# Attention scores from six part products, two heads side by side in TensorE's rows

## The reference

```python
mod = (silu(c) @ wmod).reshape(4, 6, 1, 128)           # sa, ca, ga, sb, cb, gb
h = layernorm(x) * (1 + ca) + sa
Q, K, V = split_heads(h @ W_q.T), split_heads(h @ W_k.T), split_heads(h @ W_v.T)
Q, K = rope(Q), rope(K)
score = einsum('bnqd,bnkd->bnqk', Q, K) / sqrt(8)       # causal: -inf above the diagonal
attn = softmax(score)
x = x + ga * (attn @ V).reshape(4, 1024, 128) @ W_o.T
h = layernorm(x) * (1 + cb) + sb
# shared expert + the two best of 7 routed experts per token, by softmax of h @ wr.T + rb
x = x + gb * moe(h)
```

## Time and profile before

| | us |
|---|---|
| median of three runs | 922.52 |
| the three runs | 930.70, 922.52, 921.49 |
| the profiled execution | 927.8 |
| its span, first to last instruction | 926.1 |
| ahead of the attention's first maxima | 66.1 |
| attention, quads 0 to 15 | 461.3 (95.84 to 557.12) |
| behind the attention | 369.0 |

### The profile page before, as it was taken

The page is one execution under the profiler, slowest core; times in us unless marked ns, Lnnn a source line. Parts: engine busy times, 40 slices in busy tenths (PEclk is TensorE's granted clock), DMA queues, the critical chain, the costliest instruction groups (busy, mean ns, idle before and its releaser), DMA issues.

```text
span 926.1 us, 17554 instructions
## 1 busy us (share of the span) xinstructions
PE 788.9 (85%) x5168; PEld 442.1 (48%) x5168; DVE 625.0 (67%) x1970; ACT 510.4 (55%) x969; POOL 312.4 (34%) x491
## 2 busy tenths in 40 slices
PE   3988999999999999999999997650884778999990
PEld 2551333333333333333333356540764667999880
DVE  5999678998989989998989654720592222333353
ACT  3770366666767666666667778321422444666650
POOL 1347122122111222111221114075014766666562
PEclk9995589999999999999999997795897999999995
DMA  7480311323212332113330195021112222222524
GB/s 200 117 236 23 76 29 26 53 53 53 40 21 47 53 53 53 28 28 53 53 53 3 31 181 117 3 73 41 32 40 60 66 63 65 65 67 65 152 88 142
DMA packets 59051, 62.62 MB, mean 68 GB/s; under 512 B 9097, under 2 KB 50697, under 8 KB 56649
## 3 DMA queue, kind: packets, MB, share of 16 engines
q1 hardware_dynamic: 53218, 50.04, 25.0%
q0 software_dynamic: 4480, 9.64, 2.9%
q10 hardware_dynamic: 1264, 1.84, 0.6%
HBM read 37.55 MB, written 23.55 MB: 66 GB/s over the span
## 4 chain that ended last, share of the span: by engine, by line
PE 66%; DVE 10%; another core or an unknown queue 7%; ACT 6%; issue 5%; DMA 2%; SPq 1%; POOL 1%; ACTq 1%; DVEq 0%; POOLq 0%
PE ps L1492 15%; PE ps L1545 15%; PE ps L1570 14%; PE ps L1726 6%; PE ps L1737 5%; PE ps L1747 2%; DVE junk L1082 2%; PE ps L1633 2%; PE ps L1522 2%; DVE leftmax L1086 1%; PE ps L1641 1%; DMA qa<-mparts 1%; ACT rows L856 1%; SPq L582 1%
## 5 line engine op out<-in xcount | busy, mean ns | idle before, releaser
L835 ACT ACTIVATE probs<-ps 128x1024 f32<-128x1024 f32 (+3 forms) x384 | 295.1, 813 | 181.0 <-PE ps L1570 180.6
L1082 DVE CUSTOM_DVE_ANT_0 junk<-ps,tri 128x128 f32<-128x128 f32 (+3 forms) x512 | 221.6, 486 | 31.0 <-PE ps L1492 28.9
L1492 PE MATMUL ps<-ka,qa 72*128 72x512 bf16 (+3 forms) x768 | 224.1, 348 | 3.6 <-DVE rowmax L1082 2.3
L668 POOL TENSOR_SCALAR_AFFINE_SELECT probs<-probs 128x512 f32<-128x512 f32 x128 | 81.1, 634 | 380.2 <-ACT probs L835 380.2
L1570 PE MATMUL ps<-qa,ka 75*128 75x512 bf16 (+3 forms) x768 | 192.7, 334 | 1.6 <-DMA qa<-mparts 1.5
L1545 PE MATMUL ps<-probs,v 128*32 128x512 f32 (+3 forms) x1536 | 166.5, 506 | 1.8 <-POOL probs L668 1.8
L1086 DVE TENSOR_REDUCE leftmax<-ps 128x1 f32<-128x512 f32 x256 | 162.4, 682 | 7.4 <-PE ps L1492 7.3
L1492 PEld LDWEIGHTS ps<-ka,qa 72*128 72x128 bf16 x768 | 67.2, 99 | 167.6 <-DVE rowmax L1082 65.5
L1570 PEld LDWEIGHTS ps<-qa,ka 75*128 75x128 bf16 x768 | 71.8, 100 | 81.4 <-ACT probs L835 28.8
L735 POOL DMA_INDIRECT routed_results_scratch<-y_s,s_dest x76 | 76.2, 1003 | 61.7 <-issue 56.6
L676 POOL DMA_INDIRECT slot_rows_scratch<-rows,slot x64 | 62.6, 978 | 91.6 <-DVE slot L1283 73.1
(11 more groups left out here) (183 smaller groups left out, 1003.1 us busy)
## 6 DMA issues: line engine op xcount, KB each, us to landing
qa<-q_parts_scratch SPq DMA_DIRECT2D x48, 192.0 KB
slot_rows_scratch<-cst SPq DMA_DIRECT2D x1, 5396.0 KB, 34.3
srow<-slot_rows_scratch SPq DMA_DIRECT2D x76, 71.0 KB
ka<-k_parts_scratch SPq DMA_DIRECT2D x32, 128.0 KB
q_parts_scratch<-qk_parts SPq DMA_DIRECT2D x12, 256.0 KB, 4.6
k_parts_scratch<-qk_parts SPq DMA_DIRECT2D x12, 256.0 KB, 5.4
ka<-k_parts_scratch SPq DMA_DIRECT2D x16, 192.0 KB
xs<-in_x SPq DMA_DIRECT2D x4, 512.0 KB, 10.3
```

The lines of the kernel that those rows point to most:

```text
L668: nc.gpsimd.affine_select(out=p, in_=p, compare_op=ALU.is_ge, fill=0.0, base=0, pattern=[[0, HQ], [1, T]], channel_multiplier=-1).then_inc ...
L835: nc.scalar.activation(probs[s % 4][:, 2 * h:2 * h + 2, 0:CH - q0], ps[:, 2 * h:2 * h + 2, q0:CH], ACT.Exp, scale=SCALE).then_inc(s_exp, 1)
L1082: last = V.tensor_tensor_reduce(out=junk[:, bank - 5, at:at + w], in0=src, in1=tri[:, CH - w:CH], scale=1.0, scalar=LOW, op0=ALU.add, op1= ...
L1492: last = MM(ps[:, bank, at:at + w], qa[m][0:KR, h * S + q * T:h * S + (q + 1) * T], ka[m][0:KR, h * S + k0:h * S + k0 + w], start=True, st ...
```

## The change

Six of the nine pairs of parts stay: hi by all three, mid by two, the rest by one (`RUNS`), so KR = 48 and KM = 51. The pairs mid by rest, rest by mid and rest by rest are left out of the scores. To have each run of q parts against a run of k parts in rising order, k's parts stand reversed in the scratch.

Head 2j + g of a quad now stands at rows 64 g of `qa` and `ka`, columns j x 1024: two heads share the columns, one in rows 0 to 50, one in rows 64 to 114. The products of a pair of heads follow each other, in the order that changes the half of the rows each time. `PIECES` is ordered so that the same bank of two heads comes twice in a row, and `ring_plan` puts the second into the slot of the first. A quad is loaded by 12 DMAs instead of 8, the shift rows by 6 instead of 3, the ones rows by 6 instead of 3. Maxima are stored by g first, so that the shift rows of one half lie together.

```diff
-KR = NP * NP * DK
+RUNS = ((0, NP), (0, 2), (0, 1))
+KR = sum(b - a for a, b in RUNS) * DK
 KM = KR + NP
+HG = 64
+HC = HQ // 2
-PIECES = [(h, bank) for h in range(HQ) for bank in HEAD_BANKS]
+PIECES = [(2 * j + g, bank) for j in range(HC) for bank in HEAD_BANKS for g in range(2)]
@@ ring_plan
-        slot = next((s for end, s in slots if at < end), NS * SLOTS - 1)
+        if not (kind == "max" and p % 2 and plan and plan[-1][1:] == ("max", off, p - 1)):
+            slot = next((s for end, s in slots if at < end), NS * SLOTS - 1)
@@ buffers
-            qa[m] = sb(f"qa{m}", [KM, HQ * S], BF16, at=att)
-            ka[m] = sb(f"ka{m}", [KM, HQ * S], BF16, at=att)
+            qa[m] = sb(f"qa{m}", [128, HQ * S], BF16, at=att)
+            ka[m] = sb(f"ka{m}", [128, HQ * S], BF16, at=att)
@@ ones rows
-                sp.dma_start(ka[m][KR:KM, :], ones_d.bitcast(BF16)).then_inc(s_ones, 16)
+                for g in range(2):
+                    sp.dma_start(ka[m][g * HG + KR:g * HG + KM, 0:HC * S], ones_d.bitcast(BF16)).then_inc(s_ones, 16)
@@ spill
-                        dst = scr[b * NG:(b + 1) * NG, p, :, :].rearrange("g r s -> r g s")
+                        at = NP - 1 - p if w else p
+                        dst = scr[b * NG:(b + 1) * NG, at, :, :].rearrange("g r s -> r g s")
@@ load_quad
-                w = NP * DK
-                for j in range(NP):
-                    sp.dma_start(qa[m][j * w:(j + 1) * w, :], q[0:w, :]).then_inc(s_qk_in[m], 16)
-                    mid = (j + 1) * w - j * DK
-                    sp.dma_start(ka[m][j * w:mid, :], k[j * DK:w, :]).then_inc(s_qk_in[m], 16)
-                    if j:
-                        sp.dma_start(ka[m][mid:(j + 1) * w, :], k[0:j * DK, :]).then_inc(s_qk_in[m], 16)
+                for g in range(2):
+                    at = g * HG
+                    for first, stop in RUNS:
+                        rows_in = (stop - first) * DK
+                        q0, k0 = first * DK, (NP - stop) * DK
+                        dst_q = qa[m][at:at + rows_in, 0:HC * S].rearrange("r (j s) -> r j s", j=HC)
+                        dst_k = ka[m][at:at + rows_in, 0:HC * S].rearrange("r (j s) -> r j s", j=HC)
+                        sp.dma_start(dst_q, q[g, q0:q0 + rows_in, :, :]).then_inc(s_qk_in[m], 16)
+                        sp.dma_start(dst_k, k[g, k0:k0 + rows_in, :, :]).then_inc(s_qk_in[m], 16)
+                        at += rows_in
@@ load_shift
-                for p in range(NP):
-                    sp.dma_start(qa[m][KR + p:KR + p + 1, :].rearrange("o (a t) -> o a t", t=T),
-                                 mparts[m][:, p, :]).then_inc(s_m_in[m], 16)
+                for g in range(2):
+                    for p in range(NP):
+                        row = g * HG + KR + p
+                        sp.dma_start(qa[m][row:row + 1, 0:HC * S].rearrange("o (a t) -> o a t", t=T),
+                                     mparts[m][g * HC * TB:(g + 1) * HC * TB, p, :]).then_inc(s_m_in[m], 16)
@@ bank_maxima
                 h, parts = PIECES[what]
+                h = h % 2 * HC + h // 2
@@ row_scores
-                    last = MM(ps[:, bank, at:at + w], qa[m][0:KR, h * S + q * T:h * S + (q + 1) * T],
-                              ka[m][0:KR, h * S + k0:h * S + k0 + w], start=True, stop=True)
+                    last = MM(ps[:, bank, at:at + w], qa[m][g0:g0 + KR, c0 + q * T:c0 + (q + 1) * T],
+                              ka[m][g0:g0 + KR, c0 + k0:c0 + k0 + w], start=True, stop=True)
@@ body on TensorE
-                    for h in range(HQ):
-                        if h % 2 == 0 and not (first and s == 0):
-                            pe.wait_ge(s_exp, n * (2 * NS) + 2 * s + h // 2 - 1)
-                        last = MM(ps[:, h, q0:CH], ka[m][0:KM, h * S + kb * T:h * S + (kb + 1) * T],
-                                  qa[m][0:KM, h * S + c * CH + q0:h * S + (c + 1) * CH], start=True, stop=True)
-                        if h % 2:
-                            last.then_inc(s_scores, 1)
-                            ring_entries(s * SLOTS + h // 2)
+                    for pair in range(HC):
+                        if not (first and s == 0):
+                            pe.wait_ge(s_exp, n * (2 * NS) + 2 * s + pair - 1)
+                        for g in ((1, 0) if group[0] == 0 else (0, 1)):
+                            at = pair * S
+                            last = MM(ps[:, 2 * pair + g, q0:CH],
+                                      ka[m][g * HG:g * HG + KM, at + kb * T:at + (kb + 1) * T],
+                                      qa[m][g * HG:g * HG + KM, at + c * CH + q0:at + (c + 1) * CH], start=True, stop=True)
+                            group[0] = g
+                        last.then_inc(s_scores, 1)
+                        ring_entries(s * SLOTS + pair)
```

More of the change, by code:

```diff
@@ L482, in load_quad @@
                 n, m = quad(i, r), r % 3
-                q = qs_d[bass.ds(n, 1), :, :, :].rearrange("n p (d h) s -> (n p d) (h s)", h=HQ)
-                k = ks_d[bass.ds(n, 1), :, :, :].rearrange("n p (d h) s -> (n p d) (h s)", h=HQ)
-                w = NP * DK
-                for j in range(NP):
-                    sp.dma_start(qa[m][j * w:(j + 1) * w, :], q[0:w, :]).then_inc(s_qk_in[m], 16)
-                    mid = (j + 1) * w - j * DK
-                    sp.dma_start(ka[m][j * w:mid, :], k[j * DK:w, :]).then_inc(s_qk_in[m], 16)
-                    if j:
-                        sp.dma_start(ka[m][mid:(j + 1) * w, :], k[0:j * DK, :]).then_inc(s_qk_in[m], 16)
+                q = qs_d[n].rearrange("p (d j g) s -> g (p d) j s", j=HC, g=2)
+                k = ks_d[n].rearrange("p (d j g) s -> g (p d) j s", j=HC, g=2)
+                for g in range(2):
[8 more added lines that the diff above has]
+                        at += rows_in
             def load_shift(i, r):
@@ L1500, in ring_write @@
                     if what == 0:
-                        pe.wait_ge(s_qk_in[m], (third(i, r + off) + 1) * ((3 * NP - 1) * 16))
+                        pe.wait_ge(s_qk_in[m], (third(i, r + off) + 1) * (2 * 2 * len(RUNS) * 16))
                     last = row_scores(m, bank, what)
@@ L1525, in _ @@
             pe.wait_ge(s_v_free, 2 * B)
-            pe.wait_ge(s_ones, 16 * 3)
+            pe.wait_ge(s_ones, 16 * 3 * 2)
             for k, (kind, off, what) in enumerate(PRE):
@@ L1553, in body @@
                 rbase = ring_base(i, r)
-                pe.wait_ge(s_m_in[m], (third(i, r) + 1) * (16 * NP))
-                ks = [0]
+                pe.wait_ge(s_m_in[m], (third(i, r) + 1) * (16 * 2 * NP))
+                ks, group = [0], [None]
                 def ring_entries(slot):
@@ L1562, in ring_entries @@
                         ring_write(i, r, 5 + ring_bank(i, r, k), kind, off, what)
+                        group[0] = PIECES[what][0] % 2 if kind == "max" else None
                         ks[0] += 1
                 for s, (c, kb, q0) in enumerate(STEPS):
-                    for h in range(HQ):
-                        if h % 2 == 0 and not (first and s == 0):
-                            pe.wait_ge(s_exp, n * (2 * NS) + 2 * s + h // 2 - 1)
-                        last = MM(ps[:, h, q0:CH], ka[m][0:KM, h * S + kb * T:h * S + (kb + 1) * T],
-                                  qa[m][0:KM, h * S + c * CH + q0:h * S + (c + 1) * CH], start=True, stop=True)
-                        if h % 2:
-                            last.then_inc(s_scores, 1)
-                            ring_entries(s * SLOTS + h // 2)
+                    for pair in range(HC):
[9 more added lines that the diff above has]
+                        ring_entries(s * SLOTS + pair)
                     if s >= 2:
@@ L1798 @@
         cos.astype(np.float32), sin.astype(np.float32), np.eye(128, dtype=np.float32), tri, cst,
-        np.full((NP, HQ * S // 2), 0x3F803F80, np.uint32).view(np.float32),
+        np.full((NP, HC * S // 2), 0x3F803F80, np.uint32).view(np.float32),
     ]
```

1 line of the change is left out of this document (added).

## The result

The changed kernel is slower. The median of four runs is 961.1 us (959.3 to 964.9), beside 924.5 us (921.5 to 930.7) for the kernel before: a ratio of 1.039, interval 1.033 to 1.046. The prediction said 895 us, at most 921.

A forecast was written before the change was run, and what follows sets the result against it. TensorE was taken to bound the kernel, VectorE 2.5 us behind. Ahead +1, quad 0 -4, 13 settled quads from 28.39 to 27.0 us, last two -7: -28.1 us, from 922.5 to 895 us, range 879 to 921.

The forecast's parts named there:

- The overlap: Score products of two heads in different row halves run fully at once; L1570 falls from 7.9 to 4.0 us a quad.
- TensorE below VectorE: In a settled quad TensorE's sum becomes 20.1 to 23.6 us, below VectorE's 25.7.
- VectorE's idle: VectorE's idle time in a settled quad falls from 2.5 to 1.3 us, giving 27.0 us a quad.
- the cover: At the quad's start, six pieces of maxima behind the shift keep VectorE busy about 5.3 us, leaving 0.3 us idle.
- The landing: The sixth shift-row DMA lands 4.9 us after the parts are there.
- The rival of the quad's start: Late sixth shift row starves VectorE 1.5 us more; settled quads stay at 28.2 or so, 912 us; chance 0.14.
- The clock: Rival: short TensorE waits drop the clock to 1.2 GHz, a quad there takes 38 us; five give 950; chance 0.09.
- the stretch 140 to 145: Argument against the falling clock: in this stretch of the trace TensorE was busy 3.63 of 5 us at full clock.
- fewer rows alone change nothing: Score products shrinking from 75 and 72 rows to 51 and 48 gain nothing alone; 72 and 75 stream at one rate.
- Quad 0: First quad, 38.66 us, falls to 34.7, a gain of 4, if the clock rises at the same moment.
- Quads 14 and 15: Last two quads, without some or all maxima, gain 4 and 3 us, to 22 and 24.
- Ahead of quad 0: Before the first quad, three more shift DMAs delay it by 0 to 1.8 us; +1 taken.

The follow-up runs named there:

- e11: e5 with both heads of a pair in one half of the rows, so they can't run at once: 889.6 us, ratio 1.026.
- e2: The changed kernel with each pair of score products for the exponentials issued twice: 911.9 us, ratio 1.051.
- e1: The changed kernel with three shift DMAs, each writing the row of both halves, instead of six: 879.4 us, ratio 1.011.
- e6: The changed kernel with its rows filled to 64 in each half by zeros against ones, still six shift DMAs: 877.6 us, ratio 1.014.
- e4: The kernel before with six part products instead of nine, 48 and 51 rows, one head after the other, no halves: 944.6 us, ratio 1.07.
- e0: The changed kernel run again with nothing edited, beside its variants: 911.5 us, ratio 1.049.
- e5: The changed kernel with both filled rows (64 in each half) and three shift DMAs: 859.1 us, ratio 0.992.
- e9: e5 with each piece of maxima in a slot of its own, the best version: 852.1 us, ratio 0.983.
- e8: The kernel before with its rows filled to 125 and 128, filler loaded in pieces of 48 and 8 or 5 rows: 862.8 us, ratio 0.995.

## Why the prediction was wrong

**The overlap, right for a pair.** "I take full overlap": where the two products of a pair start together they take the time of one, 0.22 us a pair, as written. But a third of L1584's products start alone, so the sum of 4.0 us a quad was the best case. e11 prices what there is.

**TensorE below VectorE, in part right at the full clock.** By its busy time it is not even below: 25.6 us of 28.7 (20.1 to 23.6 forecast), beside VectorE's 25.4 (25.7 forecast). The busy time of TensorE is modelled, and how much of the difference is real is open. That it had time to spare is shown by e2, and so is how little: near 2 us, and not the difference of two sums.

**VectorE's idle, the term that was mis-sized.** "I leave 1.3 us": it is 3.3 (28.71 - 25.41). 1.59 lie at the quad's start, 0.54 before the norm, 0.72 in two waits for maxima of L1504; the other 0.45 the list of waits does not name. The start's failed step is the cover: "Six more pieces of maxima (about 5.3 us on VectorE) lie behind the shift". The landing was right to a tenth, 4.9 us; the pieces took VectorE 4.2 us (371.62 to 375.81), as each begins before the one ahead of it has ended, and I had added their durations. So it ran dry a microsecond earlier than I had it, and the first new piece came 0.8 us after TensorE resumed and not 0.7. The rival of the quad's start gave this too little (0.14) and too kind a number: settled quads were to stay at 28.2, and they are 28.7.

**The clock, the larger part, and a rival at 0.09.** Its mechanism (waits of TensorE make the clock fall) was half of it: with the waits shorter, 57.6 us less are spent at 1.2 GHz (e1), but with the rows filled and every wait left, 109.5 us less (e6). Its price was right: the 91 us more at 1.2 GHz (117.5 for 26.4) come to 26 us by its 11 us in 38. What failed is the step that was to exclude it: "the stretch 140 to 145 has TensorE busy 3.63 of 5 us and kept the full clock". That row is from a kernel with 72 and 75 rows in use and a TensorE otherwise full; the change lowered the share of time and the rows at once, and the rows had no term in the rival. And "fewer rows alone change nothing" was weighed for the streaming rate only: e4 and e6 show that rows change the clock. The changed kernel does show what the Trainium skill (TensorE: Matmul & The Clock Gate, the section on PSUM-queue depth-cycling) describes: short waits between groups, and a clock that swings between its two levels. As a cause they aren't enough, since e6 has the same waits with its rows filled and spends 26.4 us at 1.2 GHz where e0 spends 135.9.

**Quad 0.** Forecast 34.7 us, measured 30.98 at a mean clock of 0.81. The clock first rose 8.3 us into the quad and not after the 26.4 taken over from before; two heads of 51 rows were in use there, not one of 75, and e4 with one of 51 took 152 us. That it was quick was luck for this term: nothing in the working looked for it. **Quads 14 and 15.** Forecast 22 and 24; with the clock up (e5) they are 25.14 and 26.52: gains of 1.1 and 0.7, not 4 and 3. That nearly the whole saving of TensorE would show there was the error. What holds them instead was not followed up: in e5 TensorE's busy time is 23.3 and 26.0 us there, ScalarE's 19.2 and 18.4. In the changed kernel itself they were 30.83 and 30.00, at 0.82 and 0.84.

**Ahead of quad 0** +0.5 us, forecast +1. **Behind the attention** nothing changed but 1.5 us.

The size of the failure by its parts, on the attention of e0 (501.1): filled rows alone -34.2 (e6), three shift DMAs on top of them another -17.1 (e5, 449.7), own slots another -7.1 (e9, 442.6). The parts are not independent: the shift DMAs alone brought -29.2 (e1), as they relieve the clock too. Against a kernel before with its rows filled (e8, 450.7) the change gains 1 us with both repairs and 8 with the slots: the forecast of 28 was far too large even where nothing went wrong.

**What stays open.** Why quads 0 and 1 still stand at 0.83 and 0.95 in e5 and e9 though their rows are filled, where the kernel with 128 rows for one head stands at 0.94 and 1.00 (e8); whether the filler's values matter (only zeros against ones were tried); what holds quads 14 and 15; and what the 0.4 to 0.5 us gaps before the norm would come to in another order of products.

## What to carry to other kernels

Where a change makes TensorE narrower (fewer rows) or idler, ask of its clock first: a saving that leaves the engine waiting can be taken back at 1.2 GHz, and filling unused rows with zeros cost no time in a quad here and kept the clock up but for 26.4 us. Give the kernel before the same remedy before the change is credited with it. Before trusting that another engine becomes the bound, size that engine's idle time from its gaps, one by one: overlapped durations in a timeline do not add up, and this chain of DMAs on one queue grew by its issue time (six took 3.71 us to issue, three with the same bytes in all 1.65). A wait at a seam that the bound engine used to hide is worth removing before the saving is made, as three DMAs for six did here.

## What the hardware showed that was not expected

- Rows in use act on the clock. 48 and 51 rows: three whole quads, 152 us of unbroken work at 1.2 GHz. 72 and 75 rows: 26 us. 125 and 128 rows, 53 to 77 of them filler: 1.7 to 3.2 us, quad 0 at a mean clock of 0.94 to 0.97.
- Filler rows, zeros against ones, count as rows in use: 135.9 us at 1.2 GHz without them, 26.4 with them (e0, e6).
- Two products in different halves of the rows that start together run at once in full, at 256 and at 512 columns: 0.28 and 0.39 us for two, the time of one. In one half, two of 256 take 0.39.
- The same filler bytes in DMAs of 56 and 53 rows delayed the attention's start by 39 us; in pieces of 48, 8 and 5 rows by none.
